# A fused cross-attention and feed-forward block: the preparation stage in another order, context and keys ahead of the first queries

## The reference

```python
xq  = layer_norm(x, qn_w, qn_b)
ctx = layer_norm(context, cn_w, cn_b)
q = (xq @ q_w).reshape(B, N, H, D)
kv = (ctx @ kv_w).reshape(B, M, 2, H, D)
k, v = kv[:, :, 0], kv[:, :, 1]
attn = einsum('bnhd,bmhd->bhnm', q, k) * D ** -0.5
attn = softmax(where(xa_mask[:, None], -FLT_MAX, attn))
x = x + einsum('bhnm,bmhd->bnhd', attn, v).reshape(B, N, C) @ proj_w + proj_b
h = layer_norm(x, n2_w, n2_b)
x = x + gelu(h @ fc1_w + fc1_b) @ fc2_w + fc2_b
```

## Time and profile before

| | |
|---|---|
| time, median of 3 runs | 1141.03 us |
| lowest, highest | 1140.65, 1141.56 us |
| the profiled execution | 1140.68 us, of which its span 1138.9 us |
| preparation, up to the loop's first product on PE | 61.84 us |
| PE busy, whole span | 1109.7 us |
| PE's three longest waits in the first 62 us | 3.81, 3.99 and 4.09 us |

### The profile page before, as it was taken

How to read it: one execution, slowest core, us unless ns; L and a number is a source line. 1 busy time by engine, 2 the same in 40 slices (tenths; PEclk the granted TensorE clock), 3 DMA queues, 4 the chain that set the end, 5 groups by cost and what they waited for, 6 DMA issues and landing times.

```text
span 1138.9 us, 16359 instructions
## 1 busy us (share of the span) xinstructions
PE 1109.7 (97%) x5849; PEld 947.1 (83%) x5849; DVE 576.2 (51%) x1155; ACT 398.1 (35%) x1127; POOL 234.1 (21%) x187
## 2 busy tenths in 40 slices
PE   5889999999999999999999999999999999999998
PEld 5679998999899888888888888888888888888887
DVE  5778887888888765633323322322332333232212
ACT  2455665566666654421311321221221131121110
POOL 1525335533564330100100100100110110010000
PEclk9999999999999999999999999999999999999999
DMA  7011111122111025202002002001001000100101
GB/s 245 8 16 57 57 38 38 56 91 87 39 57 39 29 69 163 74 20 74 1 1 75 1 2 74 1 1 74 1 1 55 21 1 33 42 1 1 38 1 37
DMA packets 40192, 48.76 MB, mean 43 GB/s; under 512 B 11013, under 2 KB 19245, under 8 KB 40135
## 3 DMA queue, kind: packets, MB, share of 16 engines
q1 hardware_dynamic: 37919, 43.74, 11.7%
q10 hardware_dynamic: 2216, 4.21, 1.0%
HBM read 30.54 MB, written 16.78 MB: 42 GB/s over the span
## 4 chain that ended last, share of the span: by engine, by line
PE 81%; DVE 14%; ACT 2%; issue 2%; DMA 0%; DVEq 0%; SPq 0%; ACTq 0%
PE bank L1396 31%; PE bank L1367 31%; PE bank L1273 8%; PE bank L1231 4%; DVE nmax L889 2%; PE bank L1212 2%; DVE PTl L912 2%; DVE xTl L895 1%; DVE bnst L940 1%; DVE S L882 1%; PE bank L1379 1%; DVE xhat L952 1%; DVE qTl L901 1%; DVE aTl L917 1%; PE bank L1262 1%
## 5 line engine op out<-in xcount | busy, mean ns | idle before, releaser
L1396 PE MATMUL bank<-w,gTh 128*128 128x512 f32 x1024 | 319.1, 393 | 0.0
L1130 DVE CAST gTh<-g 128x512 fp32r<-128x512 f32 x128 | 56.9, 444 | 443.6 <-ACT g L790 443.6
L790 ACT ACTIVATE g<-bank,cols 128x512 f32<-128x512 f32 x128 | 88.0, 688 | 472.6 <-PE bank L1367 471.4
L1396 PEld LDWEIGHTS bank<-w,gTh 128*128 128x128 f32 x1024 | 192.4, 188 | 42.7
L1396 PE MATMUL bank<-w,gTl 128*128 128x512 f32 x512 | 200.5, 392 | 0.0
L1367 PE MATMUL bank<-hT0h,w 128*128 128x512 f32 x512 | 162.3, 398 | 0.4 <-DVE w L1087 0.4
L1367 PE MATMUL bank<-hT1h,w 128*128 128x512 f32 x512 | 159.1, 392 | 0.1
L484 POOL TENSOR_TENSOR hrs<-hve,mhalf 128x1 f32<-128x1 f32 x32 | 17.6, 549 | 551.4 <-DVE hve L1104 551.4
L1396 PEld LDWEIGHTS bank<-w,gTl 128*128 128x128 f32 x512 | 96.2, 188 | 21.9
L1367 PEld LDWEIGHTS bank<-hT0h,w 128*128 128x128 f32 x512 | 94.7, 188 | 22.1 <-DVE w L1087 0.7
L1367 PEld LDWEIGHTS bank<-hT1h,w 128*128 128x128 f32 x512 | 95.1, 188 | 20.1 <-issue 0.8
(11 more groups left out here) (104 smaller groups left out, 1798.2 us busy)
## 6 DMA issues: line engine op xcount, KB each, us to landing
xr<-in_x SPq DMA_DIRECT2D x16, 512.0 KB, 3.4
x_scratch<-xr SPq DMA_DIRECT2D x16, 512.0 KB, 2.8
x<-x_scratch SPq DMA_DIRECT2D x8, 1024.0 KB, 5.6
out<-x SPq DMA_DIRECT2D x7, 1024.0 KB, 4.3
w1raw<-in_L_xattn_fc_w SPq DMA_DIRECT2D x16, 256.0 KB, 3.0
w2raw<-in_L_xattn_fc_w SPq DMA_DIRECT2D x16, 256.0 KB, 2.8
kvw<-in_L_xattn_kv_w ACTq DMA_DIRECT2D x2, 1024.0 KB, 9.3
qraw<-in_L_xattn_q_w ACTq DMA_DIRECT2D x4, 256.0 KB, 5.8
```

The source lines that it names most:

```text
L790: act.activation(g[:, :], bF[j % 2][:, :], ACT.Gelu, bias=cols[:, F1B + j:F1B + j + 1]).then_inc(a_gelu.sem, 1)
L1130: dve.tensor_copy(gT[HI][j % 4][:, :], g[:, :]).then_inc(v_ghi.sem, 1)
L1396: mm = pe.matmul(bC[t][:, :], gT[d][j % 4][:, t * P:(t + 1) * P], w2[:, j, w, :], start=(j == 0 and i == 0), stop=(j == JT - 1 and i == 2))
```

## The change

It rewrites the preparation of every engine; the loop and all behind it stay.

- **Loads.** The context goes first, `x` of unit 0 second. The key weights, the value weights and the projection weights move from ACT's list to SP's, and the waits for weight loads between them go.
- **PE** multiplies the identity with itself, 8 products ahead of the transpose of the norm rows and 6 behind it; nothing reads their result. Context transposes and keys come ahead of the transposes and queries of unit 0. The query bias is made with `cols` as the stationary and `qraw` as the moving operand, 4 products of 1 x 512 in place of 16 of 128 x 1; ACT copies the row to `qrow` and PE turns it into columns with 4 transposes. Each key half has its own signal. The scores of unit 0 stand between the transposes of unit 1, and the values of batch 0 come among them.
- **DVE** takes the context's statistics first. The query bias's scaling is on ACT. The projection weights' low parts (`wpl`) are spread through the softmax of unit 0.
- **POOL** clears `kbdl`, computes the context's deviation first, and clears the two halves of `vbd` after the norms of units 0 and 1. It no longer subtracts a maximum for unit 0.
- **ACT** exponentiates unit 0 head by head (32 instructions, as L667), in place of two whole tiles. `wph` is made in four pieces.

```diff
@@ sync_program
+        sp.dma_start(cx[0:M, :, :], ctx.rearrange("b m c -> m b c")).then_inc(d_ctx, 16)
         load_x(static(0))
         for i in range(3):
             load_row(sp, i)
-        sp.dma_start(cx[0:M, :, :], ctx.rearrange("b m c -> m b c")).then_inc(d_ctx, 16)
+        sp.dma_start(kvw[:, :, 0:C], kv_w[:, 0:C].rearrange("(k p) n -> p k n", p=P)).then_inc(d_kw, 16)
         load_mask(static(0))
         load_mask(static(1))
-        sp.wait_ge(d_kw, 16)
         load_x(static(1))
-        sp.wait_ge(d_vw, 16)
+        sp.dma_start(kvw[:, :, C:2 * C], kv_w[:, C:2 * C].rearrange("(k p) n -> p k n", p=P)).then_inc(d_vw, 16)
         sp.wait_ge(d_x[0], 16)
         load_x(static(2))
+        sp.dma_start(praw[:, :, :], proj_w.rearrange("(k p) n -> p k n", p=P)).then_inc(d_pw, 16)
         sp.dma_start(projb[:, :], proj_b.rearrange("(a c) -> a c", a=1).to_broadcast([P, C])).then_inc(d_projb, 16)
-        sp.wait_ge(d_pw, 16)
@@ gpsimd_program
+        pool.memset(f32(kbd[LO][:, :, :, :]).rearrange("p a b c -> p (a b c)"), 0.0).then_inc(p_zkey, 1)
...
             if prep == "q":
+                v_xhat.wait(pool, k.plus(2), UT - 1)
+                zero_values(0)
                 may_negate(k.plus(2))
                 negative(k.plus(2))
                 x_rstd()
-                for b in range(B):
-                    pool.memset(f32(vbd[:, b, :, :, :]).rearrange("p a b c -> p (a b c)"), 0.0).then_inc(p_zero, 1)
+                v_xhat.wait(pool, k.plus(3), UT - 1)
+                zero_values(1)
                 return
             if prep == "scores":
-                v_max.wait(pool, k.plus(1), 0)
-                less_max(0).then_inc(p_less0, 1)
-                v_max.wait(pool, k.plus(1), 1)
-                less_max(1).then_inc(p_less.sem, 1)
                 may_negate(k.plus(2))
                 negative(k.plus(2))
+                x_rstd()
                 probs(0)
-                x_rstd()
                 probs(1)
@@ scalar_program
-        act.dma_start(kvw[:, :, 0:C], kv_w[:, 0:C].rearrange("(k p) n -> p k n", p=P)).then_inc(d_kw, 16)
-        act.dma_start(kvw[:, :, C:2 * C], kv_w[:, C:2 * C].rearrange("(k p) n -> p k n", p=P)).then_inc(d_vw, 16)
-        act.dma_start(praw[:, :, :], proj_w.rearrange("(k p) n -> p k n", p=P)).then_inc(d_pw, 16)
...
+        def q_row():
+            act.wait_ge(t_qbias, 1)
+            act.activation(qrow[0:1, :], bank[7][0:1, :], ACT.Copy, scale=SCALE).then_inc(a_qrow, 1)
...
             if prep == "scores":
                 x_hi(0)
                 x_hi(1)
-                exp_all0()
-                exp_all(1)
-                t_scores.wait(act, s, UT * KT - 1)
+                exps(0, 0, H)
+                values_hi(0)
+                exps(1, 0, H)
                 q_hi(0)
@@ vector_program
             if prep == "rows":
-                stats()
+                ctx_stats()
+                ctx_variance()
                 columns()
+                stats((0,))
+                ctx_normed()
+                stats((1,))
                 v_bn.wait(dve, n, UT - 1)
                 variance()
-                ctx_stats()
-                normed()
-                ctx_variance()
                 return
...
             if prep == "scores":
                 for g_ in range(KT):
                     masked(0, g_)
                 maximum(0)
+                x_lo(0)
+                x_lo(1)
                 for g_ in range(KT):
                     masked(1, g_)
                 maximum(1)
-                x_lo(0)
-                x_lo(1)
-                sum_of(0).then_inc(v_esum0, 1)
                 recip(0)
-                exp_sum()
-                recip(1)
                 stats()
                 v_bn.wait(dve, n, UT - 1)
                 variance()
+                values_lo(0)
+                proj_weights(range(2))
+                recip(1)
+                proj_weights(range(2, KT))
+                normed()
                 q_lo(0)
                 q_lo(1)
-                normed()
                 values_lo(1)
-                proj_weights(range(KT))
@@ tensor_program
+        def busy(n):
+
+            for _ in range(n):
+                pe.matmul(bank[6][:, 0:P], ident[:, :], ident[:, :], start=True, stop=True)
+
+        busy(8)
         pe.wait_ge(d_rows, 16 * 7)
         pe.transpose(bank[7][:, 0:40], rows[:, :], ident[0:40, 0:40]).then_inc(t_cols, 1)
+        busy(6)
...
+            i = pe.matmul(bank[7][0:1, :], cols[:, QNB + k:QNB + k + 1], qraw[:, k, :], start=(k == 0), stop=(k == KT - 1))
...
+        def q_columns():
+            pe.wait_ge(a_qrow, 1)
             for m in range(KT):
+                i = pe.transpose(bank[7][:, 64 + m:65 + m], qrow[0:1, m * P:(m + 1) * P], ident[0:1, 0:1])
+            i.then_inc(t_qrow, 1)
```

165 lines of the change are left out of this document (90 added, 75 removed).

## The result

| | before | changed |
|---|---|---|
| median (lowest to highest), same chip, 4 runs each | 1141.30 us (1140.65 to 1142.44) | 1134.29 us (1132.25 to 1135.25) |
| ratio of the changed kernel to the one before, 95% interval | | 0.9935 (0.9918 to 0.9952) |
| the profiled execution, its span | 1140.68, 1138.9 | 1135.25, 1133.5 |
| first maximum of unit 0 ends | 42.57 us | 36.31 us |
| loop's first score | 61.84 us | 55.20 us |

The changed kernel is faster by 7.0 us between the medians, 0.65% by the ratio. The forecast was 1126 us, 15 us faster, with a range from 1121.5 to 1130.5: the sign was right, the size was more than twice what came, and the time lies outside the range. The profiled execution, 1135.25 us, is the longest of the four.

What follows compares the result with a forecast made beforehand. The preparation before the loop was taken as partly idle, partly at half clock, with PE waiting for ACT and DVE. Gains of 12.0 us up to the first maximum and 3.1 us to the loop gave 1126 us; range 1121.5 to 1130.5.

Steps and rivals of the forecast that it cites:

- The keys at 11.3 us: Start of the preparation: PE's key products begin at 11.3 us, with 13 us as the late end.
- 2.94 MB: 11.2 us: Loads at the start: 2.94 MB ahead of or beside the key weights, which are therefore there at 11.2 us.
- they end by 5.8 us, about when I expect the norm rows: PE's start: the first 8 identity products end by 5.8 us, about when the norm rows land.
- Case C: Rival, start: big loads share with `qraw`, key weights come at 13 to 15 us; 1127.7 to 1130 us; chance 0.12.
- PE from the keys on, at full clock: Keys to unit 0's queries: PE's work takes 14.1 us at full clock, queries ending at 25.4 us.
- Rival B: Start: identity products do not lift the clock, five us of work at half pace cost 2.5 us; 1128.5 us; chance 0.20.
- Maximum to loop: First maximum's end to the loop's first score: 16.2 us in place of 19.3, 3.1 us better.
- two `wpl` 1.24, the norm of unit 2 0.95: DVE's list before the loop: these take 1.24 and 0.95 us ahead of the low parts of the queries.
- The same half-clock stretch as at 61 to 65 us: Loop entry: PE idles 3.6 us, as now (4.09), so the same half clock follows and nothing is gained.
- Case D: Rival, loop entry: the clock stays up, saving 1.5 us: 1124.5 us, down to 1121.5 with shorter start gaps; chance 0.09.
- cases A to D: All the faster cases; A is the forecast itself, loop starting at 45 to 48 us, 1124 to 1127.5 us, chance 0.54.
- F: Rival, ACT's exponentials: 0.52 us a head, 5.4 us more, 1131.4 us; chance 0.03, 0.02 of it slower than before.

Runs made afterwards that it cites:

- e2: The changed kernel with 14 more identity products on PE ahead of the keys, to fill its wait for the key weights: 1133.41 us.
- e4: The changed kernel with SP waiting for the key weights before it issues `x` of unit 1 and all loads behind it: 1131.24 us.
- e5: The changed kernel again, unaltered, on another chip: 1132.11 us.
- e8: The changed kernel with unit 0's softmax as before the change (POOL subtracts, ACT takes whole tiles, DVE adds up): 1132.77 us.
- e9: The changed kernel with the query bias made by 16 products of 128 x 1 as before, at the place of the last row product: 1134.73 us.
- e6: The changed kernel with POOL multiplying one head of each tile of unit 0's probabilities in place of 16 (output not the reference's): 1129.66 us.
- e13: The changed kernel with 25 identity products on PE in the wait before the loop, once DVE has read the first values: 1128.93 us.
- e7: The changed kernel with DVE's four `wpl` ahead of the second reciprocal, then the queries' low parts, then the norm of unit 2: 1127.83 us.
- e3: The changed kernel with all four `wpl` on DVE ahead of the second reciprocal, before POOL's multiplications: 1130.75 us.

## Why the prediction was wrong

**The keys at 11.3 us (measured 12.2 to 13.7, but for the filled e2).** One failed step is "2.94 MB: 11.2 us". The rate was right: by 10.5 us the changed kernel's slices, which answer to the earlier trace rows, add up to 2.62 MB (forecast 2.65):

```profile
GB/s 0 197 290 185 268 399 408 335 348 384 389 385 386 388 253 29 0 0 0 11 2 0 5 5 0 0 0 0 11 0 17 29 32 26 26 37 15 26 40 24
```

But the key weights had landed only when the slices had moved 3.6 MB, at 13.4 us: what is issued behind them is served beside them. Holding that back (e4) still gave no better than 12.30 us, so the bytes ahead are not the whole of it; the rest of their landing time is not settled. The other failed step is "they end by 5.8 us, about when I expect the norm rows": the rows landed at 6.3 to 7.6 us, and with the six identity products, which I had priced at nothing to 0.6 us, they held the keys by themselves in e5 and e8. Case C had the first mechanism and its place (a wait of the first key row for `kvw`, 13 to 15 us); no case had the second. In every profile but e2's the keys start 0.9 to 2.4 us later than the forecast.

**Keys to maximum (19.2 us; 22.77, and 19.84 to 20.44 in nine of the eleven profiles).** The failed step is the condition "PE from the keys on, at full clock". The identity products did lift the clock in the first profile, at 6.5 us, but it was down again before the keys, which ran at half clock: 2.9 us. Rival B had this price (2.5 us), from "a wait of some 2 us for the context and the keys" among others, but it had the clock never lifted, and I gave it 0.20 and took it as an alternative to C. In the profiled execution both came true at once, the late weights of C and the half clock of B. That the one brings the other isn't shown: e9 lost the clock ahead of its wait. The other 0.7 us is a mis-sized sum.

**Maximum to loop (16.2 us; 18.89).** The step that failed is the term "two `wpl` 1.24, the norm of unit 2 0.95". They took 3.44 and 1.86 us (start to start), +3.1 us, beside POOL's multiplications; everything else in the stretch was right or 0.3 us better, the exponentials among them. I had weighed sharing between POOL and DVE, but only for the clearing of `vbd` early on, where there was slack, and not for the one place where DVE was last. Both lists were there to be read. e6 puts 2.2 us of it on the multiplications.

**The loop (0; +1.2 us).** "The same half-clock stretch as at 61 to 65 us" failed: PE idled 6.57 us instead of the 3.6 us that I had worked out, 2.7 us of it by the term above, and half clock then held to 60.5 us, 5.3 us into the loop instead of 3.1. Case D held the better outcome, and e13 shows that it was there to be had.

**What held.** The chain of terms to the end of the queries at full clock (14.1 us, measured 14.3), the 0.34 us a head, the masks and transfers of the values hidden, no cost of the extra work on idle engines, and the sign. The first clearing of `vbd` took 2.66 us beside three `wql`, in the first profile and in e5, as long as elsewhere; the 2.2 us more that the prediction considered for it did not come. The range failed because each case moved one term and left the others at their forecast, where three terms fell short together. It would have failed without the half clock at the keys too: e5, which had none, took 1132.11 us. One slip in the chances changes nothing: cases A to D add up to 0.95, and the 0.96 for "faster" takes in the 0.01 of F that is not slower.

## What to carry to other kernels

Do not count on a clock that was lifted early: in three of the four profiles in which it rose by the second identity products it was down again at or ahead of the keys. Where a case makes a wait ahead of PE longer, add a case in which the work behind it also runs at half clock; here both came in one execution. Where DVE is last, look at what POOL does in the same stretch, and put DVE's work on PSUM there and its work on SBUF elsewhere; in this kernel exchanging a few lines so (e7) was worth 4.3 us, beside 9.4 for the whole change in the same group of runs. Fill a long wait of PE with products only from a signal on, and with fewer than the shortest wait holds.

## What the runs showed of the hardware

- DVE and POOL on SBUF: two 128 x 512 `TENSOR_TENSOR` of DVE took 1.28 us beside `rstd` and 3.52 beside POOL's multiplications; two `TENSOR_SCALAR` 1.00 us in the changed kernel at 11.61 us, and up to 4.20 us (e3). POOL pays too: its small power, `rstd`, took 0.71 us at 22.80 us and 2.28 us beside `wpl` in the changed kernel.

```profile
43.94 2.28 POOL L486 TENSOR_TENSOR rstd<-veps,mhalf 128x2 f32<-128x2 f32 x1 [15.19 <-DVE veps L946]
```

- POOL's clearing of `vbd`, which writes SBUF and reads nothing there, did not get in the way of DVE's `wql`, which reads two operands in SBUF: 2.66 us for the one and 0.70 to 0.75 us for each of the others, side by side in the changed kernel.
- The clock's first rise is not the same in each execution of one kernel: the second six identity products, two rows each, took 1.60 us (full clock) in the first profile of the changed kernel and 2.93 us (half) in e5. The one that rose early had fallen again before the keys; the one that rose late had it there, and so had the six other profiles that rose late.
- A busy PE did not keep the clock up: in e9 PE was busy 4.00 of 4.00 us through the one-column products, and the granted clock was 0.50 from 25.7 us on; and 2.00 of 2.00 us from 9 to 11 us, at 0.50.
- Small loads behind large ones can land late: the last of three norm rows of 2 KB each took 4.91 us from issue to landing in e5, behind 820 KB.
